# Layer-0 attention taken by two pairs of heads at a time

## The reference, cut to what matters

```python
def _L0_attn_ref(x, gamma, w_q, w_kv, null_kv, q_scale, k_scale, w_out):   # x: 16 x 256 x 128
    xn = layernorm(x) * gamma
    q, k, v = heads(xn @ w_q), heads(xn @ w_kv)        # 16 heads of 64
    k, v = concat(null keys, k), concat(null values, v)  # 2 null keys a head
    q, k = l2norm(q) * q_scale, l2norm(k) * k_scale
    sim = q @ k.T * 8 + alibi + causal mask
    out = softmax(sim) @ v
    return out @ w_out                                  # 1024 -> 128

x = x + attn(xn) * silu(moe(xn))                        # layer 0, then layer 1 alike
```

## Time and profile before

| | |
|---|---|
| median of 3 runs | 1047.17 us (1043.44 to 1049.5) |
| span of the profiled execution | 1043.3 us |
| PE busy | 961.4 us, 92% |
| DVE, ACT, POOL busy | 692.3, 630.9, 650.4 us |
| steps 0 to 5 | about 58 to 311 us of the span |
| experts of layer 0 | about 313 to 397 us |
| steps 6 to 15 | about 397 to 795 us |

### The profile page before, as it was taken

One profiled execution on the slowest core, in us unless ns is written; L12 is line 12 of the kernel. 1 busy time (PEld: TensorE's weight loads), 2 busy tenths in 40 slices (PEclk: granted clock), 3 DMA queues, 4 the chain that ended last, 5 costly groups with the idle time before them and its releaser, 6 DMA issues.

```text
span 1043.3 us, 21426 instructions
## 1 busy us (share of the span) xinstructions
PE 961.4 (92%) x6330; PEld 690.3 (66%) x6330; DVE 692.3 (66%) x2589; ACT 630.9 (60%) x1945; POOL 650.4 (62%) x803
## 2 busy tenths in 40 slices
PE   5699989999999979999999999999998999999965
PEld 2465546666658976666665665666666788999954
DVE  6988867886673335867768768677885474345634
ACT  4458857667664557677676775766765564444442
POOL 4663787888855544667776678788746651555540
PEclk9889999999999999999999999999999999999997
DMA  9300202202427783033032030331232134787759
GB/s 296 79 7 6 42 27 66 71 26 64 113 74 188 221 233 84 10 72 81 6 66 50 22 71 26 73 67 41 52 82 52 34 102 143 227 229 226 219 168 242
DMA packets 95444, 103.19 MB, mean 99 GB/s; under 512 B 10096, under 2 KB 83031, under 8 KB 95089
## 3 DMA queue, kind: packets, MB, share of 16 engines
q1 hardware_dynamic: 88752, 89.36, 33.5%
q0 software_dynamic: 6592, 12.65, 3.5%
HBM read 77.54 MB, written 23.50 MB: 97 GB/s over the span
## 4 chain that ended last, share of the span: by engine, by line
PE 54%; DVE 18%; ACT 7%; POOL 7%; issue 6%; DMA 3%; SPq 3%; DVEq 0%; POOLq 0%; ACTq 0%
PE bank L1347 9%; PE bank L823 8%; PE bank L834 7%; PE bank L1376 7%; PE bank L1403 5%; DVE arena L2032 5%; PE bank L1391 4%; ACT arena L1759 4%; PE bank L1366 3%; PE bank L1426 3%; DVE arena L2041 3%; POOL arena L1130 2%; DVE arena L1932 2%; POOL expert_rows L655 2%; DMA arena<-in_b 1%
## 5 line engine op out<-in xcount | busy, mean ns | idle before, releaser
L1759 ACT ACTIVATE arena<-arena 128x128 f32<-128x128 f32 (+1 forms) x512 | 226.9, 446 | 96.7 <-DVE arena L2032 96.5
L2032 DVE CUSTOM_DVE_ANT_0 arena<-bank,arena 128x128 f32<-128x128 f32 (+1 forms) x512 | 183.0, 412 | 107.1 <-PE bank L1376 104.4
L1347 PE MATMUL bank<-arena 128*128 128x512 f32 x384 | 211.1, 636 | 6.0 <-ACT arena L1748 3.6
L1130 POOL TENSOR_TENSOR arena<-arena 128x512 f32<-128x512 f32 x128 | 133.4, 1045 | 121.7 <-ACT arena L1735 104.1
L2041 DVE COPY arena<-bank 128x384 f32<-128x384 f32 x256 | 130.0, 549 | 21.1 <-PE bank L1391 20.9
L1145 POOL TENSOR_TENSOR arena<-arena 128x512 f32<-128x512 f32 x128 | 129.5, 1048 | 1.3
L1735 ACT ACTIVATE arena<-bank 128x512 f32<-128x512 f32 x192 | 112.7, 588 | 27.8 <-PE bank L1347 27.5
L1391 PEld LDWEIGHTS bank<-const,arena 128*128 128x128 f32 x768 | 91.3, 142 | 56.0 <-issue 55.0
L784 POOL DMA_INDIRECT expert_out<-arena x71 | 71.1, 1002 | 90.0 <-DVE arena L923 42.1
L1376 PE MATMUL bank<-arena 64*128 64x128 f32 (+1 forms) x1024 | 119.3, 351 | 2.2 <-DVE arena L2032 1.5
L1403 PE MATMUL bank<-arena 128*64 128x256 f32 (+1 forms) x1024 | 112.2, 340 | 9.1 <-DVE arena L2041 8.7
(11 more groups left out here) (304 smaller groups left out, 1634.1 us busy)
## 6 DMA issues: line engine op xcount, KB each, us to landing
arena<-in_wp SPq DMA_DIRECT2D x40, 514.0 KB
arena<-recip_rows SPq DMA_DIRECT2D x30, 512.0 KB, 6.4
XN<-in_wp SPq DMA_DIRECT2D x24, 514.0 KB
arena<-expert_rows SPq DMA_DIRECT2D x46, 129.0 KB, 3.2
arena<-in_b SPq DMA_DIRECT2D x64, 64.0 KB
arena<-expert_out SPq DMA_DIRECT2D x16, 256.0 KB, 5.1
expert_out<-fill SPq DMA_DIRECT2D x11, 338.6 KB, 7.9
expert_rows<-fill SPq DMA_DIRECT2D x1, 2644.5 KB, 21.6
```

The lines of the kernel that those rows point to most:

```text
L1130: pool.tensor_tensor(sq[:, i % 2], r, r, ALU.mult).then_inc(S["sq_done"], 1)
L1347: mm = pe.matmul(RING[bnk][:, :], xa[:, p, t * P:(t + 1) * P], wqkv[:, 512 * k:512 * k + 512], start=True, stop=True)
L1759: ins = act.activation(w, w, ACT.Exp, bias=nm[:, p, 16 * t + h:16 * t + h + 1], scale=-1.0, accum_out=den[:, p, 16 * t + h:16 * t + h + 1])
L2032: ins = v.tensor_tensor_reduce(out=SPb[:, c % 2, 384 * k + P * t:384 * k + P * t + n], in0=SBANK[k][:, P * t:P * t + n], in1=alibi[:, h, N ...
```

## The change

Pairs are now taken two at a time. `RING_USES` has four rounds (d = 0 to 3) of three parts in place of eight pairs of two parts. In round d PE issues turn_p(2d), part 0, what belongs to pair 2d, part 1, turn_p(2d+1), what belongs to it, part 2, then scores(2d+2), scores(2d+3), weigh(2d), weigh(2d+1). The four PSUM banks are shared: an even pair has `SBANK` for its scores and for its turned probabilities, an odd pair has `TBANK`; so scores(c+2) waits until turned(c) has emptied the banks. DVE does turned(2d), turned(2d+1) and then the two rows_max of the next round; `denominators` moves from the end of a step into pair 0 of the next, `seeds` from pair 6 to pair 7, and two `sums` one pair later. ACT takes the exponentials of pairs 2d and 2d+1 in round d itself, with part 0 of the ring between the last two heads; before, it was a pair ahead.

```diff
 RING_USES = {
-    0: ([("unit", 8, 1)], [("unit", 10, 1)]),
-    1: ([("qk", 0, 1), ("qk", 1, 1)], [("unit", 0, 2), ("qk", 2, 1)]),
...
-    7: ([("unit", 11, 1)], [])}
+    0: ([("unit", 8, 1)], [("unit", 10, 1), ("qk", 0, 1)], [("qk", 1, 1), ("unit", 0, 2), ("qk", 2, 1)]),
+    1: ([("qk", 3, 1)], [("unit", 1, 2), ("qk", 4, 1)], [("unit", 2, 2), ("qk", 5, 1), ("unit", 3, 2), ("qk", 6, 1)]),
+    2: ([("unit", 4, 2)], [("qk", 7, 1), ("unit", 5, 2)], [("unit", 6, 2), ("unit", 7, 2)]),
+    3: ([("unit", 9, 1)], [("unit", 11, 1)], [])}
+NFOUR = NPAIR // 2
...
+        PAIRBANK = (SBANK, TBANK)
...  PE
-                        mm = pe.matmul(SBANK[k][:, P * t:P * t + n], qT[r:r + 64, p, c, t * P:(t + 1) * P],
+                        mm = pe.matmul(PAIRBANK[c % 2][k][:, P * t:P * t + n], qT[r:r + 64, p, c, t * P:(t + 1) * P],
...
-                for c in range(NPAIR):
-                    if c + 1 < NPAIR:
-                        pe.wait_ge(S["ttr_done"], b * 16 + (2 * c + 2))
-                        scores(p, c + 1)
...
-                        weigh(b, p, c - 1)
...
-                    ring(c, 0)
-                    turn_p(b, c)
...
+                for d in range(NFOUR):
+                    turn_p(b, 2 * d)
+                    ring(d, 0)
+                    behind_turns(2 * d)
+                    ring(d, 1)
...
+                    turn_p(b, 2 * d + 1)
+                    behind_turns(2 * d + 1)
+                    ring(d, 2)
...
+                    if d + 1 < NFOUR:
+                        for c in (2 * d + 2, 2 * d + 3):
+                            pe.wait_ge(S["pt_evac"], b * 16 + (2 * c - 2))
+                            scores(p, c)
...
+                    for c in (2 * d, 2 * d + 1):
+                        weigh(b, p, c)
...  ACT
+                for d in range(NFOUR):
+                    c = 2 * d
+                    probs(b, p, c, 0)
+                    probs(b, p, c, 1)
+                    probs(b, p, c + 1, 0)
+                    ring(d, 0)
+                    probs(b, p, c + 1, 1)
+                    if d:
+                        out_evac(b, p, d - 1)
...
+                    ring(d, 1)
...
+                    ring(d, 2)
+                    for k in (c, c + 1):
+                        if k in first:
+                            first_norm_kept(act, 4 * (k + 5 * b), 4)
...  DVE
+                for d in range(NFOUR):
+                    pair(2 * d)
+                    pair(2 * d + 1)
...
+                    if d + 1 < NFOUR:
+                        rows_max(b, p, 2 * d + 2)
+                        rows_max(b, p, 2 * d + 3)
```

More of the change, by code:

```diff
@@ L101, in step_uses @@
     if isinstance(b, int) and b >= FB + 2:
-        extra = {(1, 1): ("xt", "wt"), (3, 1): ("lg", "fold")}.get((g, part))
-    return ring_uses(g, part, more) + ([(extra[b == FB + 2], max(b - FB - 3, 0), 0)] if extra else [])
+        extra = {(0, 2): ("xt", "wt"), (1, 2): ("lg", "fold")}.get((d, part))
+    return ring_uses(d, part, more) + ([(extra[b == FB + 2], max(b - FB - 3, 0), 0)] if extra else [])
 def step_order(b):
-    return [u for g in range(NPAIR) for part in (0, 1) for u in step_uses(b, g, part)]
+    return [u for d in range(NFOUR) for part in range(3) for u in step_uses(b, d, part)]
 RING_FIRST = [("unit", u, 0) for u in range(NU)] + [("qk", 0, 0)] + \
@@ L1452, in step, with ring @@
                 g = RANK_STEP.get(b) if isinstance(b, int) else None
-                def ring(c, part):
-                    for use in step_uses(b, c, part):
+                def ring(d, part):
+                    for use in step_uses(b, d, part):
                         if use == ("unit", 0, 2):
@@ L1491, in step @@
                         null_scores(1 - p)
-                    first = null_at(b) + 1 if before else NPAIR
                     if c >= first:
@@ L1503, in step @@
                         ranks1(g, MISC)
-            def finish(b, p):
-                weigh(b, p, NPAIR - 1)
-                turn_comb(b)
+                    turn_p(b, 2 * d + 1)
+                    behind_turns(2 * d + 1)
+                    ring(d, 2)
+                    if d == 0 and before and not (isinstance(b, int) and b < 2):
+                        turn_back(b - 2, p)
+                    if d + 1 < NFOUR:
+                        for c in (2 * d + 2, 2 * d + 3):
+                            pe.wait_ge(S["pt_evac"], b * 16 + (2 * c - 2))
+                            scores(p, c)
+                    elif more:
+                        pe.wait_ge(S["ring_evac"], ring_use(b, ("qk", NQ - 1, 1)) + 1)
+                        for c in range(2):
+                            pe.wait_ge(S["pt_evac"], b * 16 + (2 * c + 14))
+                            scores(1 - p, c)
+                    if isinstance(b, int) and b == 0 and d == 0:
+                        pe.wait_ge(S["lg_read"], 1)
+                    for c in (2 * d, 2 * d + 1):
+                        weigh(b, p, c)
             def nulls():
@@ L1562, in _ @@
             logits(7)
+            scores(0, 1)
             step(0, 0, 0, before=False)
@@ L1814, in _ @@
             tokens_out(7)
-            for k in range(2):
-                probs(0, 0, 0, k)
             step(0, 0, before=False, first=(1, 2, 3, 4))
@@ L2097, in step, with pair @@
             def step(b, p, more=2, routing=False, before=True, flushed=False, x1=None):
-                for c in range(NPAIR):
+                def pair(c):
                     if routing and c == 4:
@@ L2104, in step @@
                         tables(v, link, 0, (c - 2,))
[L2105 to L2111 removed]
+                    if c == NPAIR - 2:
                         null_sub(b, p)
@@ L2133, in step @@
                     if c == 0 and before and not flushed:
+                        denominators(b - 1, 1 - p)
+                    if c == 1 and before and not flushed:
                         comb_out(b - 1)
-                    if c == 1 and before and not (isinstance(b, int) and b < 2):
-                        y_back(b - 2)
+                    if c == 3 and isinstance(b, int) and b in RANK_STEP:
+                        tile_ranks(v, link, RANK_STEP[b], MISC)
                     if c == null_at(b) and more:
                         null_scores(b + 1, 1 - p)
-                    if c == 6 and more == 2:
+                    if c == 7 and more == 2:
                         seeds(b + 2)
@@ L2178, in _ @@
             rows_max(0, 0, 0)
+            rows_max(0, 0, 1)
             for b in range(FB + 1):
                 step(b, b % 2, routing=b == 0, before=b > 0)
+            denominators(FB, FB % 2)
             comb_out(FB)
```

87 lines of the change are left out of this document (27 added, 60 removed), and 2 rows, old and new, of the table RING_USES.

## The result

The changed kernel takes 1074.82 us (median of 4 runs, 1072.91 to 1076.97) against 1047.64 of the kernel before in the same comparison: the ratio is 1.027, with an interval of 1.024 to 1.030. It is slower, as forecast, and the time lies inside the range; the size is not the forecast one: 27.2 us more in the median and 31.8 more in the profiled span (1075.1 against 1043.3), where 16 were expected.

A forecast was written before the change was run, and what follows sets the result against it. PE's work sets most steps, POOL's round trip a part of some late ones. -35.8 + 35.2 + 17.6 - 6 - 2 + 2.6 + 1.1 + 2 + 3.2 = +17.9, say +16: 1063 us, range 1036 to 1084.

The forecast's parts named there:

- The wait for the second head: PE at turn_p in each round waits for ACT's second exponential: 0.55 us, 64 times, +35.2 us.
- The saving of 0.56 us a round: Two pairs' scores and weigh side by side pay three array-mode changes once instead of twice: 35.8 us in all.
- The ring uses: PE waits for ACT to free banks in rounds 0 and 1: 1.6 us a step, steps 0 to 10, +17.6.
- The waits that vanish, -6: Waits that steps 0 to 10 have now disappear, such as 0.44 us in step 7: about 6 us.
- The seeds "just in time, at no cost": At the step's end, seeds behind the last copy leave DVE just in time for the next rows_max: no cost.
- Steps 11 to 13, -2: Counted along POOL's work, 42.9 us a step against 44.25 in step 12: -2 us for the three.
- DVE late: Rival, chance 0.13: sums waiting for POOL make DVE 0.7 us late each round, 1105 us; routing rounds only, 1078.
- Experts and step 6, +3.7: PE waits behind ACT's table load at step 6's start, +2.6, and at turn_comb ahead of the experts, +1.1.
- Step 15, +3.2: Last step: no ring work fills the second pair's turn, +1.8; turn_comb and output scaling come later, +1.4.
- the shorter chain: Rival, chance 0.22: PE waits 0.3 us instead of 0.55 each round, ring waits half; kernel gains, 1031 to 1040 us.
- Even: Rival, chance 0.12: head waits as forecast, ring waits covered by them; +4 us or less, 1047 to 1051 us.
- Half the saving: Rival, chance 0.10: each group of eight matmuls still pays for its first loads; 18 us more than forecast, 1081 us.

The follow-up runs named there:

- ring-first kernel: Changed kernel with the first ring use of each round put back between weigh and the first turn_p: ratio 1.021 to the kernel before.
- kernel with all repairs: Changed kernel, five edits: first ring use before turn_p, seeds and denominators before copies, step 6 exponentials before experts, step 5 denominators before maxima: 0.996 of kernel before.
- three edits together: Changed kernel with first ring use ahead of turn_p, seeds ahead of pair 7's copies, denominators ahead of pair 0's copies: ratio 1.003 to the kernel before.

## Why the prediction was right or wrong, point by point

- **The wait for the second head** (0.55 us, 64 times): right. From the scores, DVE starts at 1.13, ACT at 1.93, the first head's transposes at 2.97 and the second's at 3.85, where 1.12, 1.91, about 2.93 and 3.87 were added up. turn_p waits 34.3 us for ACT, in the forecast 30 to 40; but that table counts 0.33 of each 0.55. From start to start, all of turn_p in the sixteen steps took 52.5 us more than before, where 35.2 and some 6 at single places were written down; longer waits in steps 0, 1, 6, 12 and 14 and the lower clock are in the rest. It comes to this because nothing stands between weigh and turn_p; the ring-first kernel takes the wait out of rounds 1 to 3.
- **The saving of 0.56 us a round**: right in kind, too large in size. The groups save what was said (1.51 and 1.46 us for two, forecast 1.49 and 1.44), but the neighbours do not: scores and weigh together went from 13.26 to 11.86 us in step 4, counted from start to start, units and projects from 15.09 to 14.74, and the null scores rose by 0.16. That makes 0.40 a round, 1.6 a step instead of 2.2.
- **The ring uses**: oversized. In step 4 PE waits 0.25 us for a ring bank in round 1, where 1.0 was written down, and not at all in round 0, where it was 0.6. The first qk use waits 0.36 more, but for POOL, which the prediction had at nothing. These errors and the one above cancel within 0.4 us, so that a step came out at 40.63 where 41 was written down. The right length of a step was partly luck, and so is the sum of steps 0 to 10: an estimate from step 4 puts the ring term some 14 us too high over eleven steps, and the saving 10 us too high over 64 rounds.
- **The waits that vanish, -6**: not so in step 7. The 0.44 us that PE waited there before are gone, but three waits of 0.25 us for ring banks stand there instead. **Steps 0 and 1, +2** on top of two ordinary steps: together they take 2.0 us more than before in all. turn_p waits up to 2.22 us there, and waits ahead of weigh of up to 2.75 us are gone, which the prediction did not count.
- **"PE busy time falls by some 30 us"**: wrong as a sign to look for. Scores and weigh fall by 30.9, but a wait that falls inside a group is counted as its work (turn_p +19.8), and slow matmuls count in full.
- **The seeds "just in time, at no cost"**: this step of the working failed, though it cost little. It asked only whether DVE comes in time for the next maximum. It left out that POOL waits for the seeds and PE's first qk use of the next step for POOL. In the changed kernel the wait is about 0.4 us in an ordinary step (12.0 us in the table of waits, 7.4 of them one wait ahead of step 0, which the kernel before has too with 7.0), covered mostly by the wait for the second head; in the kernel before, the late seeds alone cost 1.1%.
- **The denominators in the next step**: left out but for the place ahead of the experts. Behind the first copies they run while POOL multiplies, and take 3.2 us in step 12 (672.80 to 675.99), where the kernel with all repairs takes 1.2 in step 4; turn_comb waits 6.6 us in all, and 14.2 once the wait for the heads is cut.
- **Steps 11 to 13, -2**: failed, it is +4.0. The term took POOL's loop as what sets these steps, and counted nothing for DVE between POOL and PE. In step 12, PE waits for ACT at turn_p 2.3 us, for the null scores from DVE 2.0 and for the denominators 0.8; for POOL itself 0.2. One link further back POOL does come in: a sum on DVE waits 2.64 us for POOL, and behind it stand two copies and then the null scores (700.09), for which PE waits. That a sum waits for POOL is the condition of the rival "DVE late", though it is the null scores and not the maxima that come late by it. The granted clock of the step is 0.96. Of the +4.0, some 1.6 is this lower clock: in the second execution of the changed kernel the same wait is 2.04 us, the clock stays at 1.00, and step 12 takes 45.46 us instead of 47.03. PE's timeline behind that wait, in the first execution and in the second:

```profile
700.43 0.99 PE L1419 MATMUL bank<-arena 32*128 32x256 f32 x2 [2.02 <-DVE arena L2013]
```

```profile
700.33 0.69 PE L1419 MATMUL bank<-arena 32*128 32x256 f32 x2 [2.04 <-DVE arena L2013]
```

- **Experts and step 6, +3.7 on top of an ordinary step**: the waits are right (2.16 against 2.3 at turn_comb, 3.12 against 3.1 at turn_p); the lower clock behind each, 2.75 and 2.5 us, was not thought of. Together they are the largest term that the prediction had at nothing.
- **Step 15, +3.2**: it is +5.2. turn_p waits for more than one head in rounds 0 and 1, as said, and the late turn_comb shows as a wait of 1.31 us for DVE at 802.99 (+1.4 was written down). Then comes the clock, which was not: scores of two pairs take 2.87 us at 803.49 instead of 1.51. **Step 14**: +1.3 instead of 0; its waits for ACT are 2.6 us in the table, where four ordinary rounds show 1.3.
- **The table load.** In the changed kernel ACT ends the experts' last work at 409.31, loads, and takes the first exponential at 410.63:

```profile
409.00 0.31 ACT L877 ACTIVATE RA<-RA 128x128 f32<-128x128 f32 x1 [1.19 <-DVE RA L919]
409.33 1.28 ACT L1762 ACT_TABLE_LOAD   x1
410.63 0.40 ACT L1762 ACTIVATE arena<-arena 128x128 f32<-128x128 f32 x1
```

The switch costs 1.32 us from end to start, and PE's wait is what the forecast made of 1.28. The Trainium skill ("ScalarE: Activation LUTs", section "What ACT_TABLE_LOAD costs") would have added 1.38 us for a drain; this trace does not show it.

Of the rivals, "the shorter chain" fell at its own point of decision, the 0.55 us. "Even" was right in what it supposed, head waits as forecast and hardly any ring waits, but not in the time: the smaller saving, the lower clock and steps 11 to 15 put it back. "Half the saving" holds in part, by the neighbours; its reason, that each group of eight still pays, does not, as the groups save what was said. "DVE late" had the right engine and the wrong place: it is late not with the maxima but with what other engines wait for.

So the forecast is right in its sign and in its main mechanism, the wait for the second head that eats the saving. That the amount lies near is partly luck, since terms that were too large and terms that were left out stand against each other.

## What to carry to other kernels

When a group is moved so that its data comes just too late, price the wait and also what it hides: the repair of the largest wait gave 7 us or so here, because two shorter ones stood behind it; the three edits together brought some 25. For each small step that is moved, ask which other engine waits for it and what that one feeds. Where PE would fall idle ahead of dense work, look at the granted clock behind such waits in the trace, and give that work a price range with and without the lower clock.

## What the runs showed of the hardware

- The granted clock (1.00 is 2.4 GHz, the lower level 1.2) was 0.58 and 0.66 on the mean of the windows behind waits of 2.16 and 3.12 us, and the lost time (2.75 and 2.5 us) was about as large as the waits. With waits of 0.55 us in every round, steps 4 and 7 stayed at 1.00. The length of one wait does not settle it: in the changed kernel the clock fell behind a wait of 1.31 us (803) and not behind waits of 1.67 and 1.72 us (121 and 89): the windows of 8 us around them show 0.79, 1.00 and 1.00. Around the wait of 2.0 us in step 12 they show 0.79 in one execution and 1.00 in the other.
- A change between half rows and half columns costs about 0.17 us (0.35 for two).
- The addition and the products of the denominators, DVE instructions that read two SBUF operands, take longer while POOL's large products run. In step 12 of the changed kernel:

```profile
672.80 0.21 DVE L2050 TENSOR_REDUCE arena<-arena 128x32 f32<-128x64 f32 x1
673.05 1.02 DVE L2053 TENSOR_TENSOR arena<-arena 128x32 f32<-128x32 f32 x1
674.10 0.35 DVE L2055 RECIPROCAL arena<-arena 128x32 f32<-128x32 f32 x1
674.49 1.58 DVE L2058 TENSOR_TENSOR arena<-arena 128x32 f32<-128x32 f32 x2
...
672.98 8.04 POOL L1143 TENSOR_TENSOR arena<-arena 128x512 f32<-128x512 f32 x8
```

The addition (L2053) and the two products (L2058) take 1.02 and 1.58 us against 0.22 and 0.42 in step 4 of the repaired kernel, where they end before POOL's products begin; the reduction and the reciprocal, with one operand, keep their 0.21 and 0.35. By the Trainium skill ("SBUF — State Buffer", section "SBUF: two separate sides") such a DVE instruction and a POOL instruction share a pair of ports that one of them holds for its whole length; the trace agrees, each of POOL's products being about 1.0 us long.
